# Feed-forward token loads of an AdaLN megakernel: the shifted half issued by ScalarE, the other half and the predecessors' rows by SyncE

## The reference, cut to what matters

```
def shift_token(t):
    t1, t2 = jnp.split(t, 2, axis=-1)
    t2 = jnp.pad(t2, ((0, 0), (1, 0), (0, 0)))[:, :-1]
    return jnp.concatenate([t1, t2], axis=-1)

x = x + o @ wo                        # o: local attention of shift_token(x)
h = shift_token(x)
mu = h.mean(-1, keepdims=True)
var = h.var(-1, keepdims=True)
h = (h - mu) / jnp.sqrt(var + 1e-05) * lg + lb
h = h @ w1 + b1
a, g = jnp.split(h, 2, axis=-1)
h = a * jax.nn.gelu(g, approximate=False)
x = x + h @ w2 + b2
```

## Time and profile before

| | |
|---|---|
| median of 3 runs | 1378.8 us (1377.47 to 1379.67) |
| profiled execution | 1379.28 us, its span 1377.4 us |
| TensorE busy / VectorE / ScalarE / GpSimd | 92% / 77% / 63% / 52% of the span |
| granted TensorE clock, mean | 0.977 |
| feed-forward of layer 0 | about 917 to 1012 us |
| feed-forward of layer 1 | about 1292 us to the end |

### The profile page before, as it was taken

The page is one execution under the profiler, slowest core; times in us unless marked ns, Lnnn a source line. Parts: engine busy times, 40 slices in busy tenths (PEclk is TensorE's granted clock), DMA queues, the critical chain, the costliest instruction groups (busy, mean ns, idle before and its releaser), DMA issues.

```text
span 1377.4 us, 39931 instructions
## 1 busy us (share of the span) xinstructions
PE 1264.8 (92%) x16229; PEld 986.4 (72%) x16229; DVE 1055.6 (77%) x2379; ACT 867.4 (63%) x2061; POOL 714.5 (52%) x575
## 2 busy tenths in 40 slices
PE   6769999989999999997999999987889999998887
PEld 5757888867677777765788888755558888887544
DVE  6958756558878878868999899845769999998465
ACT  5642232346666666666999999843458999997421
POOL 5422144523445444337877777712358777777010
PEclk9989999999999999998999999999999999999999
DMA  5031554102000000010000000011010000000011
GB/s 162 32 94 47 109 124 86 40 2 72 9 3 4 3 3 3 4 29 5 9 10 19 15 10 6 2 40 34 18 29 10 10 20 15 9 4 9 13 40 49
DMA packets 62044, 41.43 MB, mean 30 GB/s; under 512 B 41235, under 2 KB 51878, under 8 KB 61734
## 3 DMA queue, kind: packets, MB, share of 16 engines
q1 hardware_dynamic: 61424, 38.68, 11.4%
q10 hardware_dynamic: 438, 0.20, 0.1%
HBM read 28.10 MB, written 2.37 MB: 22 GB/s over the span
## 4 chain that ended last, share of the span: by engine, by line
PE 63%; DVE 17%; SPq 7%; ACT 6%; POOL 3%; issue 3%; DMA 0%; ACTq 0%; DVEq 0%; POOLq 0%
SPq L1878 6%; PE PS L2476 5%; PE PS L2449 4%; PE PS L1612 4%; PE PS L2460 4%; PE PS L2421 4%; PE PS L2496 4%; PE PS L2387 4%; PE PS L1621 3%; PE PS L2388 3%; PE PS L2389 3%; PE PS L590 3%; PE PS L1651 2%; DVE d_mx L1389 2%; PE PS L1599 2%
## 5 line engine op out<-in xcount | busy, mean ns | idle before, releaser
L1950 POOL TENSOR_TENSOR turn<-qk,sinl 128x1024 f32<-128x1024 f32 x64 | 215.7, 3371 | 108.1 <-DVE qk L2078 108.1
L1943 POOL TENSOR_TENSOR rn<-ss,neghalf 128x16 f32<-128x16 f32 x64 | 209.2, 3269 | 33.7 <-DVE ss L2071 33.2
L2274 ACT ACTIVATE kx<-PS,e_mx 128x128 f32<-128x128 f32 x512 | 151.2, 371 | 18.7 <-DVE e_mx L2062 18.7
L1389 DVE TENSOR_REDUCE d_mx<-PS 128x4 f32<-128x576 f32 x128 | 96.7, 755 | 55.2 <-PE PS L1612 52.7
L790 ACT ACTIVATE m_work<-PS 128x512 f32<-128x512 f32 x72 | 43.0, 597 | 121.9 <-PE PS L570 120.8
L1512 ACT ACTIVATE pa<-PS 128x512 f32<-128x512 f32 x128 | 76.4, 597 | 59.5 <-PE PS L1621 59.4
L1061 DVE TENSOR_TENSOR m_work<-m_work,PS 128x512 f32<-128x512 f32 x72 | 49.4, 687 | 69.0 <-ACT m_work L790 68.0
L2062 DVE TENSOR_REDUCE e_mx<-PS 128x8 f32<-128x1024 f32 x64 | 78.2, 1222 | 30.3 <-PE PS L2449 30.3
L1612 PEld LDWEIGHTS PS<-kx,d_q 32*64 32x64 f32 x2048 | 65.9, 132 | 47.7 <-issue 31.6
L1522 ACT ACTIVATE pm<-pm 128x512 f32<-128x512 f32 x128 | 80.7, 630 | 30.1 <-DVE pp L1394 29.4
L2476 PEld LDWEIGHTS PS<-e_vv,e_pa 128*64 128x64 f32 x2048 | 70.1, 137 | 38.1 <-issue 32.4
(11 more groups left out here) (273 smaller groups left out, 3578.1 us busy)
## 6 DMA issues: line engine op xcount, KB each, us to landing
cb<-comb_rows SPq DMA_DIRECT2D x16, 512.0 KB, 8.7
Z<-comb_rows SPq DMA_DIRECT2D x16, 512.0 KB, 9.5
zs<-Z SPq DMA_DIRECT2D x64, 32.0 KB
pa<-Z SPq DMA_DIRECT2D x16, 128.0 KB
out_x<-X SPq DMA_DIRECT2D x8, 256.0 KB, 2.5
zs<-Z SPq DMA_DIRECT2D x64, 31.8 KB
pa<-Z SPq DMA_DIRECT2D x16, 127.0 KB
X<-in_L_attn_x SPq DMA_DIRECT2D x3, 512.0 KB, 7.6
```

The source lines that it names most:

```text
L1389: chain(dve.tensor_reduce(mx[:, par, :, :], s, AX.X, ALU.max))
L1943: pool.tensor_tensor(rn[:, v % 2, :], ss[:, v % 2, :], c.neghalf[:, :], ALU.pow).then_inc(rn_ready.sem, 1)
L1950: pool.tensor_tensor(rot[:, :, :, :], x, bc(sinl[:, t, :, :], 2, H2), ALU.mult).then_inc(rot_ready.sem, 1)
L2274: last = act.activation(pm[:, v % 2, h, r, j, :], PS[:, SBANK + r, at * KEYS2:(at + 1) * KEYS2], ACT.Exp, bias=mx[:, v % 2, r, at:at + 1])
```

## The change

Nothing that is computed changes. The shifted half of a group is issued by ScalarE, in a new function `load_shifted`, which has the waits of `load_group` as its own. SP keeps the plain half, and brings the four rows from the tile before in one DMA. `stats` waits for three DMAs, no longer for six. ScalarE issues groups 0 and 1 after the attention units 24 and 25, and group g+2 in iteration g, between `gelu(g,0)` and `gelu(g,1)`.

```
@@ load_group, on SP
             sp.dma_start(zg[:, g % 2, :, 0:half], tiles[:, :, g, 0:half]).then_inc(zg_loaded[g % 2].sem, 16)
-            sp.dma_start(zg[1:P, g % 2, :, half:D], tiles[0:P - 1, :, g, half:D]).then_inc(zg_loaded[g % 2].sem, 16)
-            for b in range(B):
-                before = Z[P - 1:P, TB * b + g - 1, half:D] if g else zero[0:1, b, :]
-                sp.dma_start(zg[0:1, g % 2, b, half:D], before).then_inc(zg_loaded[g % 2].sem, 16)
+            before = tiles[P - 1:P, :, g - 1, half:D] if g else zero[0:1, :, :]
+            sp.dma_start(zg[0:1, g % 2, :, half:D], before).then_inc(zg_loaded[g % 2].sem, 16)
@@ stats, on VectorE
-            dve.wait_ge(zg_loaded[g % 2].sem, zg_loaded[g % 2].at(16 * (2 + B) * (G // 2 * L + g // 2 + 1)))
+            dve.wait_ge(zg_loaded[g % 2].sem, zg_loaded[g % 2].at(16 * 3 * (G // 2 * L + g // 2 + 1)))
@@ scalar_program
+        def load_shifted(L, g):
+            tiles = Z[:, :, :].rearrange("p (b t) d -> p b t d", t=TB)
+            act.wait_ge(resid.sem, resid.at(n(L, B * g + B - 1)))
+            if f(L, g) > 2:
+                act.wait_ge(fxn_ready.sem, fxn_ready.at(f(L, g) - 2))
+            act.dma_start(zg[1:P, g % 2, :, half:D], tiles[0:P - 1, :, g, half:D]).then_inc(zg_loaded[g % 2].sem, 16)
+
@@ rest, on ScalarE
                 for u in range(nunits):
                     attend(L, u)
+                    if u in (nunits - 8, nunits - 7):
+                        load_shifted(L, u - nunits + 8)
...
                     gelu(L, g, 0)
+                    if g + 2 < G:
+                        load_shifted(L, g + 2)
                     gelu(L, g, 1)
```

## The result

The changed kernel takes **1403.1 us** (median of 4 runs, 1394.9 to 1413.5), the kernel before 1378.9 us in the same comparison: a ratio of 1.016, with a 95% interval of 1.0123 to 1.0197. Forecast were 1398 us and a range of 1386 to 1406, so the sign and the size are as predicted; how much of the size is the change's own is worked out at the end. The profiled execution of the changed kernel took 1406.6 us, its span is 1404.7, 27.3 us longer than the span of before.

What follows compares the result with a forecast made beforehand. SP's queue, standing behind the slow shifted-half transfer, was taken as the bound. Layer 1 + 9.8, layer 0 + 9 and ScalarE + 0.5 gave + 19.3 us on 1379.28, so 1398 us as a median, range 1386 to 1406.

Steps and rivals of the forecast that it cites:

- (b): Shifted half's transfer: stays at 9.3 us whoever issues it, 9.6 us from issue to the start of stats.
- The rival in which a queue of its own makes it quick: Shifted half on ScalarE's queue: lands about 5 us from issue, TensorE sets the pace, 1355 us; chance 6%.
- the rival in which ScalarE is held: ScalarE's issues in the attention: its own DMA holds it 6.9 us each time, 1422 us; chance 6%.
- (c): Start of the feed-forward: issue moves behind gelu(0,0), so stats(2) is 7.0 us later and TensorE loses 5.7 us in layer 1.
- (d): Later feed-forward groups: a new loop of 21.3 us per two groups replaces SP's bound, against 20.75 and 22.15 us before.
- (e): TensorE in the loop: idle 4.5 us once per pair of groups, slow clock costs 1.35 to 2.3 us more, taken as 1.9.
- The rival in which the clock stays up: TensorE's pauses: no slow clock follows them, layer 1 + 4.1 us, layer 0 + 5.5, 1389 us; chance 16%.
- (a): SP's queue: about 1.3 us a group for 10.3; gain bounded by VectorE's 15.0 us and turn_z's 8.3 us of waits.
- (f): Layer 1's feed-forward summed: stats(6) + 10.7 us, - 0.9 to stats(7), nothing changed behind it, + 9.8 us.
- (g): Layer 0's feed-forward summed: stats(6) + 8.2 us, iteration 6 may add 0 to 3 us, taken as + 9 us.
- (h): ScalarE in the attention: four issues of 0.73 us into 0.76 of room, taken as + 0.5 us for all.

Runs made afterwards that it cites:

- an earlier moment: Against the changed kernel, ScalarE issues the shifted half half an iteration earlier, group 2 behind attention unit 31; 1367.8 us, ratio 0.988 to the kernel before.
- a cut: Against the changed kernel, ScalarE issues the shifted half late as two DMAs of 112 and 15 partitions; 1357.4 us, ratio 0.9825 to the kernel before.
- The late moment on SP: Against the kernel before, SP issues all three DMAs of a group, the shifted half last and only after gelu(g-2,0); 1410.0 us, ratio 1.020.
- The experiment: Against the changed kernel, TensorE does four overwritten products in five long pauses ahead of down; 1389.3 us, ratio 1.005 to the kernel before.
- The repetition on the other chip: The changed kernel, unaltered, timed again on another chip; 1400.4 us against 1383.1 of the kernel before there, ratio 1.013.

## Why the prediction was right, point by point

**(b), that the transfer stays as slow: right, and the heart of it.** Ahead of the runs this was an estimate; the only measurements behind it were the traffic and the 9.3 us of the transfer from SP. The runs show 18 GB/s at a share of 0.08 from either queue, and both ways out, an earlier moment and a cut, remove the loss. The rival in which a queue of its own makes it quick falls with the same rows. That the next DMA on SP's queue stands behind it, which I had read at L1878 (6.92 us), showed again on SP with another DMA in that place (5.72 us); ScalarE's issues took 0.66 to 0.69 us in the feed-forward, so the rival in which ScalarE is held falls too. Its next DMA was always at least 8.4 us away, so whether it would stand on ScalarE as it does on SP isn't shown.

**(c), the moment of issue: right in kind, 1.9 us too large.** `stats(2)` came 8.24 us behind the first `gelu` (1318.12 - 1309.88) for 3.13 before, + 5.1 us and not + 7.0. The step that failed is "issue 1294.1", the `gelu` and 0.6 us for its duration: ScalarE sends the DMA 0.05 us after a `gelu` starts, and for group 2 it was out before the table load ahead of the first `gelu`, 1.74 us before that `gelu`. That makes 2.3 us less; 0.4 came back with a landing of 9.98 us for 9.6.

**(d), the loop: right that it binds, too small by 1.1 and 2.0 us.** `stats` 2 to 4 and 4 to 6 of layer 1 are 24.3 and 25.2 us apart; forecast were 23.2, with the clock. The landing was the term that was mis-sized: 11.05 and 12.03 us for 9.6 + 0.4. The plain half of the next group runs beside it, and a store of the results, for group 6 two of them. SP's timeline and the windows of after show the last case, inside the transfer issued at 1355.60:

```profile
1358.12 0.66 SPq L1874 DMA_DIRECT2D pa<-Z  x1
1358.81 0.61 SPq L1876 DMA_DIRECT2D pa<-Z  x1
1359.47 2.07 SPq L1903 DMA_DIRECT2D out_x<-X  x2
```

```profile
1361.60:1362.60 1.00, 1.00 (x4) 0.45 (x3) 0.20 (x1) 0.46 (x1) 0.00 (x0) 1.00 0.81 230
...
1364.60:1365.60 1.00, 0.00 (x0) 0.00 (x0) 0.00 (x0) 0.02 (x1) 0.00 (x0) 1.00 0.08 20
```

The late moment on SP has the same transfer with nothing beside it while the next DMA stands, and there the landings are 9.51 and 9.69 us. So it takes 1.5 and 2.3 us longer with that traffic beside it; how much of that is the stores and how much the plain half was not tried apart. The earlier issue of (c) takes 0.6 us off each loop, which hid a part of it.

**(e), the clock: right in kind, too small.** Behind the three pauses `down` took 5.49, 5.41 and 4.79 us for 2.94, so 2.55, 2.47 and 1.85 us more where I took 1.9; two of them lie above my upper end of 2.3. The term of 1.9 us lies between two sizes of before. Behind 4.78 us of idle time, at a granted clock of 0.50, it was 2.3 us: an `up` that was almost wholly under the slow clock (3.63 us for 1.88) and a `down` that was so only in part (3.46 for 2.94). Behind 2.52 us it was 1.35, an `up` of 3.23 us. Here the `down` of groups 0 and 2 almost wholly is under it (1.87 and 1.84 times its time, at a granted clock of 0.50 and 0.52). The experiment gives 2.5 us for a pause in layer 1 and 3.5 in layer 0, more than `down` alone. The rival in which the clock stays up had 16%; the granted clock of 0.50 excludes it. Its price was about right in layer 1 (+ 3.4 us, for + 4.1) and wrong in layer 0 (+ 0.2 for + 5.5): there, without the clock, the relief of SP in (a) pays for the late issue almost wholly.

**(f) and (g), the sums.** Layer 1: + 5.1 for the start, + 6.8 for the two loops (49.51 us for 42.75), - 0.9 for the way from `stats(6)` to `stats(7)` (10.25 us for 11.15, as forecast), together + 11.0 for + 9.8. The two errors, of - 1.9 and + 3.1, cancel in part; that the sum came so near is to that extent luck. Layer 0: + 7.2 for + 9, with issues 9.78 to 12.36 us ahead of their `stats`. `stats(6)` came 59.0 us behind the first `gelu`, for 58.7 forecast and 50.5 before, with errors that cancel again: `stats(2)` came 2.2 us sooner than forecast, and the two loops took 23.9 and 27.2 us for 23.2 and 25.3. Behind `stats(6)` it is - 1.3 us for the + 0.8 that iteration 6 was to add.

**(h), ScalarE's time in the attention: nothing, for + 0.5.** From SP's first load of a group to the first `gelu` of layer 0 it is 173.46 us in the kernel after and 173.47 before. The issues of 0.78 us at most fit into ScalarE's room.

**The total.** In the place of the change the profile has + 18.1 us for + 19.3. The repetition on the other chip says + 17.3 in its medians; the first comparison says + 24.2. In its profiled execution what is over lies ahead of the feed-forward, most of it with the clock between 290 and 330 us; its other runs have no profile. So the forecast of + 19.3 us is nearer to the change's own cost than the + 24.2 measured first. What the prediction didn't do is price the two parts of the change apart: (a) bounded the gain from SP's relief by all that waited for SP, and set it off against the loop inside one sum. It is true for the whole, but it hides that half of the change is worth 1.6% by itself.

## What to carry to other kernels

A DMA over 127 partitions ran here at a share of 0.08, the time of about one of the 16 DMA engines, 18 GB/s for 130 KB; cutting it into 112 and 15 made queue and moment indifferent, so look at the first dimension of a slow transfer before you move it. Then ask whether anybody still waits for it: behind a late issue the cut was worth 41.6 us, on SP with the rows merged 3.8. Before a load goes to another queue, ask how far ahead the old one ran: 32 us of run-ahead on SP became none behind a `gelu`, and a transfer that nobody had waited for was suddenly in full view. And price a new pause on TensorE at more than its length: the five that were filled had cost 2.5 us each in layer 1 and 3.5 in layer 0 of slow clock besides, in all 14.5 of the 18 us.

## What the runs showed of the hardware that I had not expected

- ScalarE's sequencer didn't hold a DMA back until the instruction ahead of it had ended. The DMA behind a `gelu` went out 0.05 us after that `gelu` began (1316.67 and 1316.62), and in both layers it went out before a table load that stood ahead of both in the program (925.84 and 926.39, 1308.14 and 1308.58).
- SP's queue took one long transfer in 0.7 us, and the next DMA, where it came within that time, stood until 7.6 to 7.8 us after the long one's issue, whatever it carried: a row (6.92 us, to 1304.58), four rows (6.96, to 1307.17), a plain half that came later (5.72, to 1326.53) or a store of results (6.95 in the kernel with the late moment on SP). With the piece cut in two the same row DMA took 0.68 us.
- The long transfer, at a share of 0.08 when it ran by itself, took longer with others beside it: 9.51 to 9.69 us until `stats` with nothing beside it while SP stood, 11.05 and 12.03 with plain halves and 256 KB stores beside it (a share of 0.81 and 230 GB/s in all from 1361.60 to 1362.60).
- The length of a pause alone did not say whether the clock falls. Behind an idle time of 3.85 us (late moment on SP, 1353.00) the `down` took its 2.94 us, at a granted clock of 1.00; behind one of 2.26 us (with the pauses filled, layer 0, 974.59) it took 4.55 us, at a granted clock of 0.61.
- The granted clock between 290 and 330 us fell to 0.66 to 0.72 in five of the ten profiled executions, in code that none of the kernels changes, for 6.9 us of the span in after. What decides it stays open, and so does whether it has a part in the medians of the kernel before, which were 1378.9, 1381.2 and 1383.1 us in the three comparisons.
